# Macaron block: q and k projected transposed in two fp32r parts, head pairs on two 64-row halves, the causal mask added on VectorE, feed-forward loops unrolled

## The chip, the cores and the metric

One core of a Trainium2 chip (trn2) runs the whole program. The metric is device time in microseconds of that core. The kernel before took 1724.12 us, the median of 3 runs (1723.69 to 1725.47). Profiles are one further execution each.

## The reference

Three residual steps on x of 2 x 2048 tokens, 256 channels, all fp32:

```
x = x + 0.5 * ffn(layernorm(x))         # stage a
x = x + attention(layernorm(x))         # q, k, v projections are in stage a too
x = x + 0.5 * ffn(layernorm(x))         # stage c

ffn(x): h = relu(x @ W_fc.T)**2 (1024 wide); y = h @ W_proj.T
        mem = 0; five times: reset = mem > 1; mem = 0.9*mem + y - reset; spikes += mem > 1
        return spikes / 5
attention(x): 16 heads of 16; rope on q and k; scores = q k.T / 4, causal, softmax, @ v; then @ Wo.T + bo
```

The spikes are thresholds of y, so the products must be near fp32. The kernel therefore splits operands into a rounded high part and a rest and adds three products (high x high, high x low, low x high).

## The kernel before, in words

The program has three blocks, one after the other: `ffn_phase` with first=True (stage a), `attention_phase`, `ffn_phase` with first=False (stage c). DRAM tensors carry results between them.

**Feed-forward.** Tokens go in 8 chunks of 512 (4 tiles of 128, T). Each engine runs a software pipeline: `pipeline` calls body(n, has) for each chunk number, the middle of it as a hardware loop (Fori). A body has 8 turns f, one for each 128 of the 1024 hidden columns. On PE, turn f does `up` (6 matmuls of 512 columns, L569) and, three turns late (LAG), `down` (12 matmuls of 256 columns, L583). ScalarE takes relu and square (L313 to L322), VectorE subtracts the rounded part (h_lo, L450), counts spikes of the chunk before (L417) and does the layer norms (L376 to L399). Every engine executes in order; semaphores with the names in the wait calls tie them. In stage a the norm of the finished chunk ("mid"), its transposition (tps) and the projections stand in the same turns, placed by the table FROM: `qkv` projects one quarter (128 tokens) of q and k, 512 columns, then v, 256 columns, into one bank of gps; ScalarE copies it out; GpSimd rotates (rope, L520, L525) token-major; ScalarE and GpSimd and VectorE split it in three bf16 parts (L297, L546, L300, L474); PE transposes the parts in 48 matmuls of 128 columns a chunk (`fill`, L603), ScalarE copies these (L274) and issues their stores (L289). The pipeline is 5 turns of the outer loop deep, so it has 5 more bodies than chunks.

**Attention.** A group is four heads of one batch, 8 groups. Queries go in 4 steps j of 512, keys in blocks b of 128, so step j has 4j+4 blocks, 40 a group. On PE a block has: finds (L1066: q against up to 512 keys, into one of two buffers m_ps, read by VectorE's row maximum L983; 160 a group, and they run 20 blocks ahead of the scores), scores for head pairs (L1101, two matmuls of 512 columns into s_ps[hp], with the negated maximum as extra rows of q against rows of ones in k), and products with v (L1121, into o_ps; two block numbers behind; v_w is fp32 and the tile has 32 columns a head). Where the keys of a find end at the diagonal, an extra matmul (L1069) adds the mask. ScalarE does exp (L963), GpSimd zeroes above the diagonal (L936). Contraction rows: q and k have six part products of 16 rows, bf16, 96 rows (KR), and 3 rows of maxima parts. `place_units` distributes the 160 finds over block numbers -20 to 19 by cost. In a block, `some(quarter)` deals its finds in four portions; the order is some(0), scores 0, some(1), scores 1, some(2), products half 0, some(3), products half 1. A find waits until VectorE has read the buffer of the find two before.

The maxima of a step are negated and split (L992 to L1006), turned by PE (L1077), copied (L1014), and SP writes them to rows 96 to 98 of qT by three DMAs (`shift`, L873). SP also issues the loads of the next group's q and k (31 DMAs a group) and the stores.

Of the kernel before, what the change touches and what calls it, by code (L numbers as in the profile page):

```python
# [13 lines left out]
P = 128  # L14
# [20 lines left out]
QS, KS = (0, 0, 1, 1, 0, 2), (0, 1, 0, 1, 2, 0)  # L35
NT = len(QS)
KR = NT * D
KC = KR + 3
# [32 lines left out]
def ffn_phase(nc, first, src, dst, w, io, shared):  # L71
# [19 lines left out]
    with ExitStack() as ctx:  # L91
# [13 lines left out]
        ident, identb = sb("ident", [P, P]), sb("identb", [P, P], BF16)  # L105
# [13 lines left out]
        if first:  # L119
            xm = sb("xm", [P, T, E])  # L120
            mstats, mmv, mln = sb("mstats", [P, T, 6]), sb("mmv", [P, T, 2]), sb("mln", [P, 6, T])
            qk, rq, rest = (sb(n, [P, T, 2 * E]) for n in ("qk", "rq", "rest"))
            prod = sb("prod", [P, 4, E])
            parts = sb("parts", [P, T, 3, 2 * E], BF16)
            qkT = sb("qkT", [P, 12, CH], BF16)
            v = sb("v", [P, T, E])
            cosb, sinb = sb("cosb", [P, TOK // P, 2, D // 2]), sb("sinb", [P, TOK // P, 2, D // 2])

            staged = [rest[:, :, :].rearrange("p t n -> p (t n)"), qk[:, :, :].rearrange("p t n -> p (t n)"),
                      rq[:, 0:3, :].rearrange("p t n -> p (t n)")]  # L130
# [9 lines left out]
        gpsb = [gps[:, g, :].bitcast(BF16) for g in range(2)]  # L140
# [3 lines left out]
        names += ["const_in", "w_hi", "w_lo", "identb_ok", "x_in", "res_in", "up_done", "relu_done", "hi_done",  # L144
                  "sq_done", "lo_done", "down_done", "y_evac", "spike", "sum_done", "sum_out"]
        names += ["pre_" + n for n in norm_steps]
        if first:
            names += ["mid_" + n for n in norm_steps]
            names += ["qk_done", "qk_evac", "v_done", "v_evac", "v_out", "rope_mul", "rope_done",
                      "p0_done", "p1_done", "rest_done", "p2_done", "fill_done", "fill_evac", "qkT_out0", "qkT_out1"]  # L150
# [4 lines left out]
        passed, passed_dve, passed_sp, passed_act = (sem("passed" + x) for x in ("", "_dve", "_sp", "_act"))  # L155
        CONSTS = 16 * (3 if first else 2)

        FROM = {"qkv": 2, "rope": 3, "p0": 5, "rest": 6, "p1": 7, "fill": 8}
        FILLS = 2 * T
        FB = 12 // 2  # L160
# [9 lines left out]
        def turn_of(what, f):  # L170

            return (3 if f >= FROM[what] else 4), (f - FROM[what]) % FC

        def pipeline(eng, body):

            lo, hi, end = (5, NC - 1, NC + 5) if first else (3, NC - 2, NC + 3)
            for n in range(lo):
                body(n, lambda k: 0 <= n - k < NC)
            with eng.Fori(lo, hi) as it:
                body(it, lambda k: True)  # L180
            for n in range(hi, end):
                body(n, lambda k: 0 <= n - k < NC)
# [4 lines left out]
        def _(sp):  # L187
# [15 lines left out]
            if first:  # L203
                for tab, name in ((cosb, "cos"), (sinb, "sin")):
                    sp.dma_start(tab[:, :, :, :], w[name].rearrange("(t p) (k i) -> p t k i", p=P, k=2))\
                      .then_inc(s["const_in"], 16)
                load_weight(1)
                load_weight(2)

            def hold(name, value):  # L210

                if not isinstance(value, int) or value > 0:
                    sp.wait_ge(s[name], value)
                    if not isinstance(value, int):
                        sp.sem_inc(passed_sp, 1)

            def load_chunk(c):
                if first:
                    hold("pre_norm", c)
                else:  # L220
                    hold("a_T", c)
                    sp.dma_start(ain[:, :, :], rows(io["attn"], c)).then_inc(s["a_in"], 16)
                    hold("xb_done", c)
                sp.dma_start(xin[:, :, :], rows(src, c)).then_inc(s["x_in"], 16)

            def body(it, has):
                if has(-1 if first else -2):
                    load_chunk(it + (1 if first else 2))
                if has(2):
                    hold("sum_done", it - 2)  # L230
                    if not first:
                        hold("x2_out", 16 * (it - 1))
                    sp.dma_start(xres[:, :, :], rows(src if first else io["x2"], it - 2)).then_inc(s["res_in"], 16)
                if first and has(4):
                    hold("v_evac", T * (it - 3))
                    sp.dma_start(rows(io["v"], it - 4), v[:, :, :]).then_inc(s["v_out"], 16)
                if not first and has(-1):
                    hold("x2_done", it + 2)
                    sp.dma_start(rows(io["x2"], it + 1), x2[:, :, :]).then_inc(s["x2_out"], 16)
                if has(2):  # L240
                    hold("sum_done", it - 1)
                    sp.dma_start(rows(dst, it - 2), xsum[:, :, :]).then_inc(s["sum_out"], 16)

            if not first:
                load_chunk(1)
                wait(sp, "x2_done", 1)
                sp.dma_start(rows(io["x2"], 0), x2[:, :, :]).then_inc(s["x2_out"], 16)
            pipeline(sp, body)
            wait(sp, "sum_out", 16 * NC)
            if first:  # L250
                wait(sp, "v_out", 16 * NC)
                wait(sp, "qkT_out0", 48 * NC)
                wait(sp, "qkT_out1", 48 * NC)
# [4 lines left out]
        def _(act):  # L258
# [4 lines left out]
            def high(which, c, hi, bank=tps):  # L263

                wait(act, which + "_T", c + 1)
                act.activation(hi[:, :, :], bank[:, :, :], ACT.Copy).then_inc(s[which + "_hi"], 1)  # L266

            def fill_evac(c, i):

                t, half = divmod(i, 2)  # L270
                wait(act, "fill_done", FILLS * c + i + 1)
                if i in (0, T):
                    wait(act, f"qkT_out{i // T}", 48 * c)
                act.activation(qkT[:, FB * half:FB * (half + 1), t * P:(t + 1) * P],  # L274
                               gpsb[1][:, 0:FB * P].rearrange("p (k n) -> p k n", k=FB), ACT.Copy)\
                    .then_inc(s["fill_evac"], 1)

            def v_evac(c, t):
                wait(act, "v_done", T * c + t + 1)
                wait(act, "v_out", 16 * c)  # L280
                act.activation(v[:, t, :], gps[:, 0, 0:E], ACT.Copy).then_inc(s["v_evac"], 1)

            def store_parts(c, half):

                wait(act, "fill_evac", FILLS * c + T * (half + 1))
                act.sem_inc(passed_act, 1)
                n = CH // 2
                for a in range(3):
                    act.dma_start(io["qkT"][a].rearrange("(k p) n -> p k n", p=P)[:, :, bass.ds(c * CH + half * n, n)],  # L289
                                  qkT[:, 4 * a:4 * a + 4, half * n:(half + 1) * n]).then_inc(s[f"qkT_out{half}"], 16)  # L290

            def part(c, t, k):

                if k == 0:
                    wait(act, "rope_done", 2 * (T * c + t + 1))
                    wait(act, "fill_done", FILLS * (c - 1) + 2 * t + 2)
                    act.activation(parts[:, t, 0, :], rq[:, t, :], ACT.Copy).then_inc(s["p0_done"], 1)  # L297
                else:
                    wait(act, "rest_done", T * c + t + 1)
                    act.activation(parts[:, t, 1, :], rest[:, t, :], ACT.Copy).then_inc(s["p1_done"], 1)  # L300

            def body(it, has):
                for f in range(FC):
# [19 lines left out]
                    if first and has(2) and f == 5:  # L323
                        std("mid", it - 2, mln)
# [5 lines left out]
                    if first:  # L330
                        for which, what in enumerate(("p0", "p1")):
                            k, i = turn_of(what, f)
                            if f % 2 == 1 and has(k):
                                part(it - k, i // 2, which)
                        k, i = turn_of("qkv", f)
                        if f % 2 == 1 and has(k):
                            if i < FC - 1:
                                v_evac(it - k, i // 2)
                        elif has(k):
                            c, t = it - k, i // 2  # L340
                            wait(act, "qk_done", T * c + t + 1)
# [882 lines left out]
```

## Time and profile before

| what | value |
|---|---|
| runs | 1723.69, 1724.12, 1725.47 us |
| profiled execution | 1728.13 us, its span 1726.4 us |
| PE busy | 1505.3 us, 87% |
| PE weight loads busy | 828.1 us, 48% |
| VectorE (DVE) busy | 1200.0 us, 70% |
| ScalarE (ACT) busy | 947.9 us, 55% |
| GpSimd (POOL) busy | 353.9 us, 21% |
| mean granted TensorE clock | 0.933 of 2.4 GHz |

Busy shares are means over three stages. On the time line stage a ends near 411 us, attention proper begins at 504 us and ends near 1468 us, and stage c takes the rest. Idle of an engine that nobody waits for costs nothing; the prediction thus goes by stages and by who waits for whom.

### The profile page before, as it was taken

The page shows a single profiled execution, that of the slowest core. Times are in us where ns is not written, and L with a number is a line of the kernel's source. Part 1 is how long each engine was busy: PE and PEld are TensorE (multiplying, and loading weights), DVE is VectorE, ACT ScalarE, POOL GpSimd, SP SyncE. Part 2 cuts the span into 40 slices and gives each one's busy share as a digit, 9 for nine tenths or more (in the row PEclk, how much of TensorE's full clock was granted, in tenths as well). Part 3 has the DMA queues.
Part 4 walks back from the last instruction along what each step waited for, and adds up shares of the span by engine and source line. Part 5 has one row for each costly group of instructions (what it writes and reads, how often), then busy time and mean ns, then how long its engine had stood idle before and what let it go on. Part 6 is the DMA issues. An engine that isn't in the chain of part 4 may idle for free. (4 is left out here: it accounts for less than half of the span.)

```text
span 1726.4 us, 32516 instructions
## 1 busy us (share of the span) xinstructions
PE 1505.3 (87%) x11104; PEld 828.1 (48%) x11104; DVE 1200.0 (70%) x2269; ACT 947.9 (55%) x1332; POOL 353.9 (21%) x378
## 2 busy tenths in 40 slices
PE   5989888671489999998999989999999999599997
PEld 4877777551123333332333333333333333499996
DVE  4687766740478888886888877877887880366776
ACT  5656666562015555554555645555555568266654
POOL 0046656896001011011011020020010101101000
PEclk9999989885559999999999999999999999699999
DMA  4112222326352042052051070060150000322221
GB/s 117 60 39 71 83 73 74 105 79 122 37 62 32 5 62 36 5 73 26 5 79 19 5 94 5 5 93 5 19 81 6 4 8 5 111 74 86 97 73 62
DMA packets 130140, 90.54 MB, mean 52 GB/s; under 512 B 50625, under 2 KB 126401, under 8 KB 129985
## 3 DMA queue, kind: packets, MB, share of 16 engines
q1 hardware_dynamic: 104640, 75.92, 22.3%
q10 hardware_dynamic: 25344, 12.59, 2.4%
q8 instruction: 93, 1.52, 0.4%
q14 instruction: 63, 0.51, 0.1%
HBM read 54.53 MB, written 33.55 MB: 51 GB/s over the span
## 5 line engine op out<-in xcount | busy, mean ns | idle before, releaser
L983 DVE TENSOR_REDUCE maxes<-m_ps 128x1 f32<-128x512 f32 (+3 forms) x1280 | 743.6, 608 | 220.5 <-PE m_ps L1069 113.1
L963 ACT ACTIVATE probs<-s_ps 128x1024 f32<-128x1024 f32 (+3 forms) x640 | 540.8, 894 | 390.6 <-PE s_ps L1101 389.5
L1066 PE MATMUL m_ps<-kT,qT 96*128 96x512 bf16 (+3 forms) x1280 | 457.7, 369 | 102.3 <-DVE maxes L983 45.4
L1121 PE MATMUL o_ps<-probs,v_w 128*32 128x256 f32 (+2 forms) x4352 | 345.9, 393 | 0.3 <-POOL probs L936 0.3
L1101 PE MATMUL s_ps<-qT,kT 99*128 99x512 bf16 (+3 forms) x1280 | 341.1, 352 | 2.1 <-ACT probs L963 1.7
L1066 PEld LDWEIGHTS m_ps<-kT,qT 96*128 96x128 bf16 x1280 | 122.3, 97 | 443.4 <-DVE maxes L983 279.3
L936 POOL TENSOR_SCALAR_AFFINE_SELECT probs<-probs 128x512 f32<-128x512 f32 x128 | 81.3, 635 | 936.7 <-ACT probs L963 936.7
L1101 PEld LDWEIGHTS s_ps<-qT,kT 99*128 99x128 bf16 x1280 | 109.7, 99 | 107.1 <-issue 27.0
L1121 PEld LDWEIGHTS o_ps<-probs,v_w 128*32 128x32 f32 x4352 | 87.5, 108 | 132.5 <-issue 119.7
L1069 PE MATMUL m_ps<-maskb,identb_b 128*128 128x128 bf16 x512 | 116.6, 230 | 0.0
L520 POOL TENSOR_TENSOR prod_a<-qk_a,cosb_a 128x256 f32<-128x256 f32 x64 | 69.5, 1085 | 168.1 <-ACT qk_a L343 167.9
L450 DVE TENSOR_TENSOR h_lo_a<-hsq_a,h_hi_a 128x512 fp32r<-128x512 f32 x64 | 49.8, 780 | 68.7 <-ACT h_hi_a L322 68.7
L450 DVE TENSOR_TENSOR h_lo_c<-hsq_c,h_hi_c 128x512 fp32r<-128x512 f32 x64 | 51.4, 804 | 55.2 <-ACT h_hi_c L322 54.3
L313 ACT ACTIVATE relu_c<-ups_c 128x512 f32<-128x512 f32 x64 | 38.2, 596 | 76.5 <-PE ups_c L569 75.9
L611 PE MATMUL gps_a<-proj_hi_a,mT_hi_a 128*128 128x256 f32 (+1 forms) x128 | 51.2, 400 | 32.1 <-ACT qk_a L343 16.9
L313 ACT ACTIVATE relu_a<-ups_a 128x512 f32<-128x512 f32 x64 | 38.3, 598 | 69.3 <-PE ups_a L569 61.8
L583 PE MATMUL yps_a<-down_hi,h_hi_a 128*128 128x256 f32 x256 | 73.3, 286 | 2.6 <-ACT y_a L307 2.4
L583 PE MATMUL yps_c<-down_hi,h_hi_c 128*128 128x256 f32 x256 | 72.3, 282 | 0.0
L583 PE MATMUL yps_a<-down_lo,h_hi_a 128*128 128x256 f32 x256 | 71.9, 281 | 0.0
L583 PE MATMUL yps_c<-down_lo,h_hi_c 128*128 128x256 f32 x256 | 71.7, 280 | 0.0
L583 PE MATMUL yps_a<-down_hi,h_lo_a 128*128 128x256 f32 x256 | 71.6, 280 | 0.0
L583 PE MATMUL yps_c<-down_hi,h_lo_c 128*128 128x256 f32 x256 | 71.4, 279 | 0.0
(138 smaller groups left out, 2228.1 us busy)
## 6 DMA issues: line engine op xcount, KB each, us to landing
qkT_parts<-qkT_a ACTq DMA_DIRECT2D x48, 256.0 KB, 2.9
qT<-qkT_parts SPq DMA_DIRECT2D x192, 64.0 KB, 4.5
kT<-qkT_parts SPq DMA_DIRECT2D x48, 256.0 KB, 6.0
xin_a<-in_x SPq DMA_DIRECT2D x8, 512.0 KB, 4.2
xres_a<-in_x SPq DMA_DIRECT2D x8, 512.0 KB, 5.2
x<-xsum_a SPq DMA_DIRECT2D x8, 512.0 KB, 4.4
v_tok<-v_a SPq DMA_DIRECT2D x8, 512.0 KB, 3.0
v_in<-v_tok SPq DMA_DIRECT2D x8, 512.0 KB, 7.2
```

What stands on the lines that cost most here:

```text
L313: act.activation(relu[:, f % 2, :], ups[:, f % 2, :], ACT.Relu).then_inc(s["relu_done"], 1)
L450: dve.tensor_tensor(h_lo[:, f % HB, :], hsq[:, f % 2, :], h_hi[:, f % HB, :].bitcast(F32), ALU.subtract).then_inc(s["lo_done"], 1)
L520: pool.tensor_tensor(prod[:, 2 * half + m, :].rearrange("p (k h i) -> p k h i", k=2, h=H), x[:, :, :, :, m], table(tab), ALU.mult).then_in ...
L583: last = pe.matmul(yps[:, t, :], h[:, f % HB, t * P:(t + 1) * P], wt[:, f, :], start=(f == 0 and i == 0 and t % 2 == 0), stop=(f == FC - 1 ...
L611: last = pe.matmul(out, x[:, c, t * P:(t + 1) * P], wt[:, c, c0:c1], start=(i == 0), stop=(i == 3 * EC - 1))
L936: pool.affine_select(out=tile, in_=tile, compare_op=ALU.is_ge, fill=0.0, base=0, pattern=[[0, G], [1, P]], channel_multiplier=-1).then_inc ...
L963: act.activation(probs[:, b % PBUF, 2 * hp:2 * hp + 2, off:CH], s_ps[hp][:, :, off:CH], ACT.Exp)\
L983: dve.tensor_reduce(maxes[:, j % 2, h, t, k:k + 1], m_ps[:, u % 2, 0:width], AX.X, ALU.max)\
L1066: mm = pe.matmul(m_ps[:, u % 2, 0:width], q, kT[dn % 2][0:KR, h, k * CH:k * CH + width], start=True, stop=(k < j))
L1069: mm = pe.matmul(m_ps[:, u % 2, width - P:width], identb[:, :], maskb[:, :], start=False, stop=True)
L1101: mm = pe.matmul(s_ps[hp][:, h, off:CH], kT[dn % 2][0:KC, 2 * hp + h, b * P:(b + 1) * P], qT[dn % 2][0:KC, j, 2 * hp + h, off:CH], start=T ...
L1121: mm = pe.matmul(o_ps[VW * h:VW * (h + 1), start:end], v_w[dn % 2][:, b, h, :], probs[:, b % PBUF, h, start:end], start=(b == 0), stop=(b ...
```

## The change

- Stage a: q and k are projected transposed (weights stationary, tokens moving, 512 columns): first q's two halves of head dimensions, then k's, then v as before. VectorE multiplies by cos and sin from a table (`rot`, 128 x 3 x 2048), GpSimd adds and subtracts, ScalarE rounds to fp32r, GpSimd subtracts the rest. No PE transposition of q and k remains. SP stores all parts, as fp32.
- Attention: q and k have two parts, three products of 16 rows, 48 rows, in fp32r, and 2 rows of maxima parts. Heads of a pair lie at partitions 0 and 64 (HR = 64). The mask is a [128, 512] tile; a diagonal find's maximum is one VectorE operation that adds it and takes the maximum. The scale of 1/4 is in the exp. VectorE transposes the maxima in 32 x 32 blocks; 16 DMAs put them in place.
- The products of a block are one piece of up to 512 columns instead of two halves with a find between.
- Both feed-forward loops are unrolled; SP's loads and stores are in another order. Stage a's pipeline has 3 more bodies than chunks.

```
-QS, KS = (0, 0, 1, 1, 0, 2), (0, 1, 0, 1, 2, 0)
+QS, KS = (0, 0, 1), (0, 1, 0)
 KR = NT * D
-KC = KR + 3
+KC = KR + 2
...
         def pipeline(body):
+            for n in range(NC + (3 if first else 2)):
                 body(n, lambda k: 0 <= n - k < NC)
...
     SP, start of stage a: cos and sin loads leave; after the weights:
+                sp.dma_start(table[:, :, :], w["rot"]).then_inc(s["table_in"], 16)
...
     PE, stage a:
+            def project_pair(c, x):
+                if x == 0:
+                    wait(pe, "mid_evac", c + 1)
+                    wait(pe, "v_evac", c)
                 else:
+                    wait(pe, "turn_done", 4 * c + 2)
+                for ab in range(2):
+                    n0 = (2 * x + ab) * P
+                    (six matmuls: gps[:, ab, :] <- wt[:, k, n0:n0 + P], x_[:, k, :])
+            def project_v(c):
+                wait(pe, "turn_done", 4 * c + 4)
+                for t in range(T):
+                    last = project(gps[:, t // 2, (t % 2) * E:(t % 2 + 1) * E], t, 2 * E, 3 * E)
...
+                    f == 0: project_pair(it - 3, 1)    (behind down, ahead of up(it, 0))
+                    f == 3: project_v(it - 3)
+                    f == 4: wait mid_norm; turn(xm, "mid_T")
+                    f == 6: project_pair(it - 2, 0); then turn(xn)
...
     VectorE, stage a:
+            def turn_pair(c, x):
+                wait(dve, "proj_done", 3 * c + x + 1)
+                wait(dve, "rot_done", 4 * c + 2 * x)
+                for m in range(2):
+                    dve.tensor_tensor(turned[:, m], gps[:, :, :], table[:, m:m + 2, t0:t0 + CH], ALU.mult)
+                    f == 1: mid statistics;  f == 2: turn_pair(it - 3, 1), last in its turn
+                    f == 3: mid norm;  f == 5: low mid;  f == 7: turn_pair(it - 2, 0), last in its turn
...
     GpSimd, stage a:
+            def rotate(c, x):   two subtract/add of 128x512, then qk_lo (128x1024)
...
     attention, VectorE:
+                if k < j:
+                    dve.tensor_reduce(out, m_ps[:, u % 2, 0:width], AX.X, ALU.max).then_inc(max_read, 1)
+                else:
+                    dve.wait_ge(max_read, FREE_M + len(UNITS) * n + u - 1)
+                    dve.sem_inc(passed_max, 1)
+                    dve.tensor_tensor_reduce(masked[:, u % 2, 0:width], m_ps[:, u % 2, 0:width], mask[:, CH - width:CH], 1.0, NEG,
+                                             ALU.add, ALU.max, out).then_inc(max_read, 1)
...
     attention, PE:
-                if k == j:
-                    mm = pe.matmul(m_ps[:, u % 2, width - P:width], identb[:, :], maskb[:, :], start=False, stop=True)
+                pe.matmul(m_ps[:, u % 2, 0:width], qT[dn % 2][r0:r0 + KR, j, h // 2, t * P:(t + 1) * P],
+                          kT[dn % 2][r0:r0 + KR, h // 2, k * CH:k * CH + width], start=True, stop=True)
...
-                    for half in range(2):
-                        if b >= 2:
-                            products(i, dn, j, b - 2, half)
-                        if half == 0:
-                            some(3)
+                    if b >= 2:
+                        products(i, dn, j, b - 2)
+                    some(3)
...
     attention, SP:
+                for a in range(2):
+                    for par in range(2):
+                        for r in range(P // VW):
+                            sp.dma_start(out[:, :, r, :].bitcast(F32), shiftT[c0:c0 + G * T // 2, :]).then_inc(shift_in, 16)
-                    load(i, dn + 1, (2 * j, 2 * j + 1))
+                    load(i, dn + 1, (j,))
...
     attention, start: VectorE sets rows of kT[0] to 1 and the mask to 0; SP waits for both
+            sp.wait_ge(ones_ok[0], 2)
             load(0, 0, range(NT))
```

## Rows read from the trace of the kernel before

**Rows 1.** Windows, attention: us, PE, PEld, DVE, ACT, POOL busy, PEclk, DMA

```profile
604.00:690.00 86.00, 82.63 (x674) 30.43 (x673) 70.03 (x134) 50.54 (x62) 9.95 (x13) 1.00 0.35 49
```

**Rows 2.** Order of time, ScalarE, stage a: start us, us, engine, line, operation

```profile
237.44 1.03 ACT L307 ACTIVATE y_a<-yps_a 128x1024 f32<-128x1024 f32 x1
...
282.50 1.03 ACT L307 ACTIVATE y_a<-yps_a 128x1024 f32<-128x1024 f32 x1
...
320.91 1.03 ACT L307 ACTIVATE y_a<-yps_a 128x1024 f32<-128x1024 f32 x1
```

**Rows 3.** Order of time, SP and PE, from stage a to the first score

```profile
411.65 0.35 SPq L848 DMA_DIRECT2D ident_b<-in_ident  x1
...
447.50 0.26 PE L1066 MATMUL m_ps<-kT,qT 96*128 96x128 bf16 x1 [41.45 <-DMA kT<-qkT_parts]
...
504.63 0.63 PE L1101 MATMUL s_ps<-qT,kT 99*128 99x512 bf16 x1
```

**Rows 4.** Chain that ended last, stage c: start us, us, what

```profile
1506.54 2.75 PE ups_c L569 x12
...
1522.19 2.83 PE yps_c L583 x24
```

**Rows 5.** Order of time, PE, one full key block

```profile
809.14 0.39 PE L1066 MATMUL m_ps<-kT,qT 96*128 96x512 bf16 x1
...
810.45 0.38 PE L1066 MATMUL m_ps<-kT,qT 96*128 96x512 bf16 x1
...
810.76 0.64 PE L1121 MATMUL o_ps<-probs,v_w 128*32 128x256 f32 x8
...
811.33 0.39 PE L1066 MATMUL m_ps<-kT,qT 96*128 96x512 bf16 x1
...
812.28 0.39 PE L1066 MATMUL m_ps<-kT,qT 96*128 96x512 bf16 x1
```

**Rows 6.** Order of time, PE and DVE, a block with a whole product

```profile
586.02 1.06 PE L1121 MATMUL o_ps<-probs,v_w 128*32 128x512 f32 x8
587.02 0.50 PE L1066 MATMUL m_ps<-kT,qT 96*128 96x512 bf16 x2
...
587.45 1.02 DVE L983 TENSOR_REDUCE maxes<-m_ps 128x1 f32<-128x512 f32 x2 [0.89 <-PE m_ps L1066]
588.19 0.39 PE L1066 MATMUL m_ps<-kT,qT 96*128 96x512 bf16 x1 [0.62 <-DVE maxes L983]
...
588.62 2.00 DVE L983 TENSOR_REDUCE maxes<-m_ps 128x1 f32<-128x512 f32 x3
```

**Rows 7.** DMA issues (KB each, us to landing); order of time, DVE, start

```profile
rest_a<-in_up SPq DMA_DIRECT2D x1, 1024.0 KB, 6.6
...
26.63 1.40 DVE L376 BATCH_NORM_STATS2 stats_a<-xin_a 128x6 f32<-128x256 f32 x4
```

**Rows 8.** Order of time, ScalarE and DVE, stage c, turn f = 7

```profile
1577.21 0.60 ACT L313 ACTIVATE relu_c<-ups_c 128x512 f32<-128x512 f32 x1 [1.88 <-PE ups_c L569]
...
1580.50 1.22 DVE L417 SCALAR_TENSOR_TENSOR count_c<-y_c,count_c 128x1024 bf16<-128x1024 f32 x1
```

**Rows 9.** Forms of instructions: out<-in xcount | busy us, mean ns | idle before

```profile
L983 DVE TENSOR_REDUCE maxes<-m_ps 128x1 f32<-128x512 f32 x896 | 600.7, 689 | 138.4 <-PE m_ps L1066 92.7 <-PE m_ps L1069 34.3
...
L546 POOL TENSOR_TENSOR rest_a<-rq_a,parts_a 128x512 f32<-128x512 f32 x32 | 41.3, 1293 | 9.1 <-ACT parts_a L297 9.1
...
L434 DVE TENSOR_TENSOR x_c<-gps_c,xb_c 128x1024 f32<-128x1024 f32 x8 | 9.8, 1225 | 11.9 <-PE gps_c L611 11.9
```

**Rows 10.** Line L873 (min/median/max ns); order of time around a shift

```profile
L873 SPq DMA_DIRECT2D qT<-shiftT x96: 502/582/1659, 468.3 to 1428.8; - x96
DMA to landing us min/median/max: 1.6/1.7/3.2
...
687.95 0.17 DVE L1006 TENSOR_TENSOR negparts<-negrest,negparts 128x16 bf16<-128x16 f32 x1
...
698.62 0.60 PE L1101 MATMUL s_ps<-qT,kT 99*128 99x512 bf16 x2
```

More of the change, by code:

```diff
@@ L153, in ffn_phase @@
         s = {n: sem(n) for n in names}
[L155 to L160, printed above, removed]
+        passed_dve = sem("passed_dve")
+        CONSTS = 16 * (1 if first else 2)
         def rows(ap, c):
@@ L168, in wait, with pipeline @@
                 eng.wait_ge(s[name], value)
[L170 to L181, printed above, removed]
+        def pipeline(body):
+            for n in range(NC + (3 if first else 2)):
                 body(n, lambda k: 0 <= n - k < NC)
@@ L244, in _, with load_x, load_attn @@
[L244 to L248, printed above, removed]
+                sp.dma_start(table[:, :, :], w["rot"]).then_inc(s["table_in"], 16)
+            def load_x(c):
+                wait(sp, "pre_norm" if first else "xb_done", c)
+                sp.dma_start(xin[:, :, :], rows(src, c)).then_inc(s["x_in"], 16)
+            def load_attn(c):
+                wait(sp, "a_T", c)
+                sp.dma_start(ain[:, :, :], rows(io["attn"], c)).then_inc(s["a_in"], 16)
@@ new lines, in load_rest, with store_sum, store_x2 @@
+            def load_rest(c):
+                wait(sp, "sum_done", c)
+                if not first:
+                    wait(sp, "x2_out", 16 * (c + 1))
+                sp.dma_start(xres[:, :, :], rows(src if first else io["x2"], c)).then_inc(s["res_in"], 16)
+            def store_sum(c):
+                wait(sp, "sum_done", c + 1)
+                sp.dma_start(rows(dst, c), xsum[:, :, :]).then_inc(s["sum_out"], 16)
+            def store_x2(c):
+                wait(sp, "x2_done", c + 1)
+                sp.dma_start(rows(io["x2"], c), x2[:, :, :]).then_inc(s["x2_out"], 16)
@@ L265, in high @@
                 wait(act, which + "_T", c + 1)
+                if which == "mid":
+                    wait(act, "proj_done", 3 * c)
                 act.activation(hi[:, :, :], bank[:, :, :], ACT.Copy).then_inc(s[which + "_hi"], 1)
[L268 to L276, printed above, removed]
@@ L292, in part, with v_evac @@
[L292 to L300, printed above, removed]
+            def v_evac(c):
+                wait(act, "proj_done", 3 * c + 3)
+                wait(act, "v_out", 16 * c)
+                act.activation(v[:, :, :], gps[:, :, :].rearrange("p g (t e) -> p (g t) e", e=E), ACT.Copy)\
+                    .then_inc(s["v_evac"], 1)
@@ L659, in body @@
                         up(it, 0)
-                    if first and f == 0 and has(4):
-                        qkv(it - 4, FC - 1)
-                    if first and f == 0 and has(3):
-                        wait(pe, "mid_norm", it - 2)
-                        turn(xm, "mid_T")
                     if not first and f == 5 and has(-2):
@@ L1157, in body @@
                     for b in (last - 2, last - 1):
-                        for half in range(2):
-                            products(i, dn, j, b, half)
+                        products(i, dn, j, b)
                     turn_sum(i, dn, j, True)
-            pe.wait_ge(const_ok, 2)
-            pe.wait_ge(ones_ok, 6)
+            pe.wait_ge(const_in, 32)
             for x in range(MAX_FROM, 0):
```

488 lines of the change are left out of this document (208 added, 280 removed).

## The prediction

> **What bounds the kernel now.** I read the page first, then windows, chain, forms and time-ordered instructions. TensorE is the page's busiest engine, but its reasons differ by stage. In 86 us of the attention VectorE (DVE in the rows) is busy 70 and PE nearly all of the time [rows 1]. A full key block shows a closed cycle on PE: find at 809.14, find at 810.45, half products, find with mask, half products, next block's find at 812.28, thus 3.14 us [rows 5]. (A find is the 512-column score matmul whose row maximum VectorE takes.) A find stands between the two half products, and VectorE has only two m_ps buffers to read from. Where a product is already whole (the first key block of a query step), the reader sees another order: the product holds PE 1.00 us, VectorE stands 0.89 us, and PE's following find then waits 0.62 us for VectorE [rows 6].
>
> The first stage runs until 411.65, although its last feed-forward result is read at 320.91: a tail of 90.7 us. Its chunks take 45.1 us apiece late in the loop [rows 2, 3], while feed-forward matmuls alone would need 8 x (1.38 + 1.41) = 22.3 us per chunk [rows 4]. Then 35.9 us pass until attention's first find, and 57.1 us more until its first score [rows 3]. The last feed-forward stage follows PE's chain and keeps its arithmetic.
>
> The profiled execution took 1728.1 us for a span of 1726.4; the median of the runs is 1724.1, thus 4 us less. Differences worked out in the span are applied to the median.
>
> **Start, +6.** Cosine and sine loads of 0.25 MB each, and the wait of PE and ScalarE for them, leave; that is worth about 2 us. A 3.1 MB table is put on SP's queue before chunk 1's x. A 1 MB weight load took 6.6 us with 0.5 MB ahead of it [rows 7], thus about 230 GB/s at best: 3.1 MB is 14 us. VectorE takes the chunk's statistics at 26.6 us [rows 7], and what is queued up to it totals 7 MB, 31 us or more. Behind this wait stand the remaining h_lo subtractions of VectorE, and behind those PE. Net +6, bounds 0 and +14.
>
> **First stage, loop, -16.** PE per chunk afterwards: feed-forward 22.3, the q and k pairs 24 matmuls of 512 columns at 0.23 = 5.5, v 24 of 256 at 0.118 = 2.8, sixteen transposes about 2.0: 32.7 us. The 48 small transposes and their ScalarE copies leave. But only one PSUM pair serves all three projections. The second pair waits for VectorE's rotation products of the first, queued at f = 7 behind low, h_lo and a spike count. In the last stage the same queue can be read: the relu after up(7) starts at 1577.21, the spike count at 1580.50 [rows 8]. The count costs 1.14 and two 1024-element products (1.225 each [rows 9], a little overlapped) 2.4: done, with 0.2 from matmul to relu, 7.1 us after up(7). PE has two down groups, 2.8 us, in the meantime and stands 4.3. The v projection waits for the second pair's rotation, queued behind sum and both norms' statistics: about 2.5. The y copy adds 0.8. Period 32.7 + 7.6 = 40.3 against 45.1. Five chunks have this form, of which the last is cheaper before as well (38.4), and the first of them is slightly dearer: I take 16 us, bounds 0 and 30. Unrolling removes only loop branches, less than 2 us per turn, and is inside this.
>
> **First stage, tail, -37.** After the last y: count and norm of chunk 6 and 7, two transposes, two pairs and two rotations for each. Walked by order: y to chunk 6's second rotation 22 us, norm of 7 and transposes and splits 8, first pair 5 (at 1.2 GHz), rotation 2.4, second pair 5, rotation 2.4, GpSimd's two 512-column steps 2.4 (1.29 each at most [rows 9]), high part 1.0, low part 2.4, four DMA issues and landing 4. About 53 to 54 us against 90.7, since the token-major rope (six GpSimd operations per quarter chunk) is gone. Bounds -20 and -50. GpSimd is not busy enough in the loop to matter.
>
> **Boundary, -1.** 31 loads become 19 with rows of 2 and 8 KB in place of 1 and 4; bytes stay 3.6 MB. They filled most of 35.9 us before. Now VectorE must first set 2 x 4096 elements of kT (at the element rate of the adds in rows 9 4.3 us each, 9.2 with the mask) and SP stands behind it. With 25 us for the loads the sum is 35, bounds -9 and +9.
>
> **Finds ahead of the first score, -3.** Of the 57.1 us [rows 3]: no mask matmuls, ScalarE copies or PE turn of the shift; bounds -8 and +5.
>
> **Attention proper, +30.** This is the largest term. The numbers follow find d, the one after the product: VectorE starts 0.43 later (587.02 to 587.45). Its reductions follow each other every 0.655 (three in 2.00, one being 0.69) and each holds its buffer 0.69. Find c of the next block starts 0.05 after find a's reduction ends (588.14 to 588.19) [rows 6, 9]. From find to product 0.31, product to find 1.00 [rows 5, 6]. With four finds per block: 0.43 + 0.655 + 0.69 + 0.05 + 0.31 + 1.00 = 3.14 us. So the merged product gives back everything that PE saves, whatever the score pairs cost. With five finds there are two behind the product: 3.79, against 3.14 + 0.23 = 3.37 before. Per head group: four such blocks, +1.7. Fp32r finds at 0.23 instead of 0.215 lie beside. Some ten blocks with few finds stay bound by PE and gain one switch, the mask and perhaps parallel scores, about 0.25 each: -2.5. Masked maxima: 64 per group, half on the cycle, each with a further semaphore instruction and an accumulator. No row shows this custom operation. A PSUM plus SBUF add of 1024 elements takes 1.225 us, so 512 take 0.69, as the reduction does [rows 9]: lower bound 0 extra (less is excluded, it reads the same columns). Upper bound is a second small VectorE operation and its spacing, 0.35 (the subtraction of 0.17 and its spacing of 0.2 [rows 10]). I take 0.15, near to the small operation's duration: 64 x 0.5 x 0.15 = +4.8. Sum +4.0 per group, and 7.5 groups run with finds: +30. Bounds: 105 less (rival A) and 90 more (rival B).
>
> A rule speaks against the masked maxima. The Trainium skill, VectorE: DVE Perf Modes, section Two Vector instructions with no wait between them, says that an operation that also writes its accumulator is two instructions. No run here shows it. It is what the slower rival would be.
>
> **Shifts, +4.** Three DMAs become sixteen, at 0.50 to 0.58 us an issue [rows 10]. For the last query step the parts are ready at 688.1 and the first score starts at 698.6 [rows 10]. Sixteen issues and 1.7 landing are 9.7 to 11.0 us, in a window of 10.5, perhaps a little shorter now. PE's whole queue stands behind it. 0 to 1.5 us, eight times: +4, bounds 0 and +12. The two loads and one store that share SP's queue have gone out before.
>
> **Rest, -2.** In the last 20 blocks without finds ScalarE's two exponentials set the pace, -1. Final stage: the same PE order, -1; if its hidden loads come late, +5.
>
> **Sum.** 6 - 16 - 37 - 1 - 3 + 30 + 4 - 2 = -19; 1724 - 19 = **1705 us**.
>
> **Rival A, packing pays.** Two 64-row score matmuls run at once, and the finds too; then PE would need 4 x 0.23 + 2 x 0.23 + 1.0 + 0.2 = 2.6 us per block. For it: the eight product instructions of four 32-column tiles end in 0.57 us, so tiles do overlap here [rows 5]. Against it: the cycle above holds no score, and the already whole products stand with VectorE idle. If find latency proves less than 0.43 or finds slip beside products, 0.5 us x 7.5 x 28 blocks = 105 less: 1705 - 105 = 1600. Chance 0.12. The Trainium skill, TensorEngine Tiling (Array Packing), section Theoretical Speedup, allows up to 2x for at most 64 rows; the 0.57 us agree that packing occurs.
>
> **Rival B, slower.** VectorE's masked maximum is dear. Place: L983's 512 diagonal units. Break-even: 19 us over 7.5 x 32 = 240 on the cycle, 0.08 beyond my 0.15, so from 0.23 each. At 0.35: 240 x 0.20 = +48, 1753 us. For it: an added instruction, an added wait and a second output. Against: VectorE idles 16 of 86 us [rows 1], which hides extras off the cycle. If three quarters of the 480 lie on it at 0.35, 126 us in place of 36: +90, 1795. Chance 0.27.
>
> **Rival C, the first stage gives nothing.** Its new waits (4.3 and 2.5) grow by a missed turn of the in-order queues, and the table delays more. Loop and start then cost instead of give: 20 us back, 1725. Chance 0.13. The forecast has 0.48.
>
> **Range and chances.** A measurement cannot tell changes under 0.2%, 3.4 us. Forecast alone: 1685 to 1722. The range, 1640 to 1775, takes in most of B and the near side of A. Faster: A 0.12, forecast 0.44, C 0.03, thus 0.59. Same: C 0.06, forecast 0.02. Slower: B 0.27, C 0.04, forecast 0.02, thus 0.33.
>
> **What would show it.** Phase 1 ends near 365, chunks of 40 us, PE waiting at the second pair and the v projection. First find near 400. In full blocks VectorE idle about 0.8 us behind each whole product, though PE waits for maxes. Masked maximum of 512 columns at about 0.7 to 0.85. Wrong if blocks fall under 2.9 us, if masked maxima exceed 0.95, or if the tail keeps more than 70 us.

## The result and the profile after

The kernel after takes 2059.2 us (2050.6 to 2065.1, 4 runs) where the one before took 1724.4: a ratio of 1.194, 95% interval 1.189 to 1.198. The forecast was 1705, the range ended at 1775: wrong in sign and far outside. The profiled run took 2065.1 us for a span of 2063.3.

The page of the profile after, part 1, two rows of part 2 (tenths of busy time and of the granted TensorE clock in 40 slices):

```profile
PE 1750.3 (85%) x8384; PEld 941.1 (46%) x8384; DVE 1196.7 (58%) x2719; ACT 869.6 (42%) x1160; POOL 220.9 (11%) x202
...
PE   6888787249989998988989888998899999869997
...
PEclk9999898655555756665665655577575565879999
```

The clock row of before, from its page:

```profile
PEclk9999989885559999999999999999999999699999
```

PE is as busy as before by its share, but the clock row stands at 5 to 7 from the eighth slice to the 34th. Before, only the three slices ahead of the first scores had a 5, and those from the 13th to the 34th a 9. PE's busy time in the span grew from 1505 to 1750 us, although 2,720 of its instructions are gone. So PE works at 1.2 GHz, the lower of the two levels, for most of the attention. Windows by stage (us, busy time of PE, PEld, DVE, ACT, POOL, PEclk, DMA share, GB/s):

```profile
0.00:382.00 382.00, 297.94 (x1664) 259.61 (x1664) 249.82 (x451) 164.48 (x261) 85.49 (x51) 0.92 0.31 100
382.00:450.00 68.00, 10.53 (x21) 5.72 (x21) 16.99 (x44) 0.44 (x1) 15.72 (x8) 0.50 0.58 81
450.00:1790.00 1340.00, 1202.56 (x5132) 467.39 (x5135) 772.77 (x1942) 557.45 (x659) 95.39 (x131) 0.60 0.18 24
```

The attention has 0.60 in place of the 1.00 of [rows 1] (0.99 from 600 to 1400 us of before). Instructions in order of time, after: the bounds of the stages on SP and PE, a full key block at 1.2 GHz, and the wait for the last shift.

```profile
390.63 0.36 SPq L796 DMA_DIRECT2D ident_b<-in_ident  x1
400.17 0.36 SPq L798 DMA_DIRECT2D mask_b<-in_mask  x1
...
435.83 0.48 PE L1021 MATMUL m_ps<-kT,qT 48*128 48x128 f32 x2 [55.39 <-DMA qT<-qkT_parts]
...
498.23 1.12 PE L1041 MATMUL s_ps<-qT,kT 50*128 50x512 f32 x2
...
732.39 1.93 PE L1058 MATMUL o_ps<-probs,v_w 128*32 128x512 f32 x8
734.26 0.79 PE L1021 MATMUL m_ps<-kT,qT 48*128 48x512 f32 x2
734.85 0.63 PE L1041 MATMUL s_ps<-qT,kT 50*128 50x512 f32 x2
735.84 0.79 PE L1021 MATMUL m_ps<-kT,qT 48*128 48x512 f32 x1 [0.36 <-DVE maxes L943]
735.92 1.14 PE L1041 MATMUL s_ps<-qT,kT 50*128 50x512 f32 x2
736.51 0.72 PE L1021 MATMUL m_ps<-kT,qT 48*128 48x512 f32 x1
737.15 1.93 PE L1058 MATMUL o_ps<-probs,v_w 128*32 128x512 f32 x8
...
1767.03 1.22 PE L1041 MATMUL s_ps<-qT,kT 50*128 50x512 f32 x4 [5.88 <-DMA qT<-shiftT]
```

The whole product holds PE 1.87 us instead of 1.00, and the block takes 4.76 us (732.39 to 737.15) in place of 3.14 [rows 5]. The score pair starts 0.08 us behind a find (735.84, 735.92): matmuls in different 64-row halves do overlap. VectorE's part, by forms (count, busy us, mean ns, idle before):

```profile
L943 DVE TENSOR_REDUCE maxes<-m_ps 128x1 f32<-128x512 f32 x768 | 510.0, 688 | 250.6 <-PE m_ps L1021 246.2
...
L948 DVE CUSTOM_DVE_ANT_0 masked<-m_ps,mask_b 128x512 f32<-128x512 f32 x128 | 86.9, 690 | 83.7 <-PE m_ps L1021 82.0 <-DVE maxes L943 0.3
...
L948 DVE DVE_READ_ACCUMULATOR2_ANT maxes<- 128x1 f32 x512 | 42.5, 83 | 0.0
```

Reductions cost what they did [rows 9]; most of VectorE's idle time before them now ends with PE (246.2 of 250.6 us). Cut at PE's first score and at PE's first transposition of the last stage, the two profiled spans compare as follows (us):

| | before | after | difference |
|---|---|---|---|
| start to last y | 320.9 | 332.1 | +11.2 |
| last y to end of the first stage | 90.7 | 58.6 | -32.1 |
| to the first find | 35.9 | 45.2 | +9.3 |
| to the first score | 57.1 | 62.4 | +5.3 |
| attention, first score to last stage | 974.0 | 1315.4 | +341.4 |
| last stage | 247.8 | 249.7 | +1.9 |

Everything ahead of the attention nets -6. The question is the 341.

### The profile page after: what moved, and what is told of

It is laid out like the page before. It is cut to its first block and busy times, and to the rows that moved or that the text cites. A ratio compares the mean times of both kernels' runs of the same rounds, so it can differ in the third digit from the quotient of the medians.

```text
span 2063.3 us, 27094 instructions
## 1 busy us (share of the span) xinstructions
PE 1750.3 (85%) x8384; PEld 941.1 (46%) x8384; DVE 1196.7 (58%) x2719; ACT 869.6 (42%) x1160; POOL 220.9 (11%) x202
## 5 line engine op out<-in xcount | busy, mean ns | idle before, releaser
L1021 PE MATMUL m_ps<-kT,qT 48*128 48x512 f32 (+3 forms) x1280 | 662.2, 643 | 189.2 <-DVE maxes L943 61.8
L943 DVE TENSOR_REDUCE maxes<-m_ps 128x1 f32<-128x512 f32 x768 | 510.0, 688 | 250.6 <-PE m_ps L1021 246.2
L1021 PEld LDWEIGHTS m_ps<-kT,qT 48*128 48x128 f32 x1280 | 284.3, 262 | 796.7 <-DVE maxes L943 282.8
L1058 PE MATMUL o_ps<-probs,v_w 128*32 128x512 f32 (+3 forms) x2560 | 467.4, 818 | 0.2 <-POOL probs L895 0.2
L1041 PE MATMUL s_ps<-qT,kT 50*128 50x512 f32 (+3 forms) x1280 | 452.1, 552 | 7.9 <-DMA qT<-shiftT 5.9
L948 DVE CUSTOM_DVE_ANT_0 masked<-m_ps,mask_b 128x384 f32<-128x384 f32 (+3 forms) x512 | 244.9, 490 | 315.0 <-PE m_ps L1021 305.0
L1041 PEld LDWEIGHTS s_ps<-qT,kT 50*128 50x128 f32 x1280 | 223.2, 273 | 31.1 <-ACT probs L918 22.2
L1058 PEld LDWEIGHTS o_ps<-probs,v_w 128*32 128x32 f32 x2560 | 59.8, 129 | 105.3 <-issue 78.8
L436 DVE TENSOR_TENSOR h_lo_c<-hsq_c,h_hi_c 128x512 fp32r<-128x512 f32 x64 | 45.0, 703 | 62.2 <-ACT hsq_c L310 35.7
L494 POOL TENSOR_TENSOR rot_a<-turned_a 128x512 f32<-128x512 f32 x32 | 46.9, 1484 | 176.8 <-DVE turned_a L420 176.8
L574 PE MATMUL gps_a<-mT_hi_a,proj_hi_a 128*128 128x512 f32 x64 | 33.3, 520 | 33.8 <-DVE turned_a L420 29.0
```

The source lines that it names most:

```text
L436: dve.tensor_tensor(h_lo[:, f % HB, :], hsq[:, f % 2, :], h_hi[:, f % HB, :].bitcast(F32), ALU.subtract).then_inc(s["lo_done"], 1)
L494: pool.tensor_tensor(rot[:, x, m, :], turned[:, m, 0, :], turned[:, m, 1, :], op)\
L943: dve.tensor_reduce(out, m_ps[:, u % 2, 0:width], AX.X, ALU.max).then_inc(max_read, 1)
L948: dve.tensor_tensor_reduce(masked[:, u % 2, 0:width], m_ps[:, u % 2, 0:width], mask[:, CH - width:CH], 1.0, NEG, ALU.add, ALU.max, out).th ...
L1021: pe.matmul(m_ps[:, u % 2, 0:width], qT[dn % 2][r0:r0 + KR, j, h // 2, t * P:(t + 1) * P], kT[dn % 2][r0:r0 + KR, h // 2, k * CH:k * CH + ...
L1041: mm = pe.matmul(s_ps[hp][:, h, off:CH], kT[dn % 2][HR * h:HR * h + KC, hp, b * P:(b + 1) * P], qT[dn % 2][HR * h:HR * h + KC, j, hp, off: ...
```

## Experiments

Theory R: a matmul over 48 to 50 rows of the array leaves the granted clock low, where 96 to 99 rows raise it. Rivals: theory T (fp32r operands in place of bf16) and theory G (PE's gaps, made by whole products and VectorE). "Low" below is the time at 1.2 GHz in the attention, summed over windows of 10 us from their PEclk; "attention" is cut as in the table above. Before has 31 us low and 974.0; after 1015 low and 1315.4. Another start of the windows moves "low" by some 10 us. Where a pair of numbers is in brackets behind a ratio, it is the 95% interval.

**Run 1, 96 rows in one tile.** The row group of each pair's second head moves from row 64 to row 48, the shifts to rows 96 and up. What comes out is the attention of the sum of two heads' scores, and two matmuls no longer lie in different halves of the array.

```
-  r0 = HR * (h % 2);  q, k rows r0:r0 + KR              # finds, 48 rows
+  q, k rows 0:96
-  rows HR * h:HR * h + KC                               # scores, 50 rows
+  rows 0:98
```

> The kernel after, with both heads of a pair in one full-height tile: finds contract 96 rows (48 of each head) and scores 98, where after they contract 48 and 50 in a 64-row half. Number type (fp32r), instruction counts, waits and loads stay; what is computed is the attention of the sum of the two heads' scores, so the output is another one. Theory R (the granted TensorE clock falls because finds and scores fill few rows of the array): the clock of the attention rises from about 0.60 to 0.95 or more, and the time falls from 2059 to 1735 to 1790 us. Theory T (it falls because the operands are fp32r in place of bf16) and theory G (it falls because PE has gaps around the whole product and the masked maxima): clock stays near 0.6, time 2040 to 2080 us.

Measured: 1835.7 us (1828.7 to 1844.1); attention 1102.5, low 123. Its window:

```profile
600.00:1400.00 800.00, 726.83 (x3783) 364.67 (x3781) 567.42 (x1409) 412.69 (x485) 72.45 (x98) 0.95 0.26 33
```

With 96 and 98 rows the clock is back and 224 us of the loss are gone. T falls as the main cause, since this is fp32r. So does G, since the products are whole and the maxima masked. The rows and the packing changed together here; run 2 changes the rows in unpacked tiles. The expected time was missed by 46 us; run 12 takes that up.

**Run 2, before with 48 rows.**

```
-QS, KS = (0, 0, 1, 1, 0, 2), (0, 1, 0, 1, 2, 0)
+QS, KS = (0, 0, 1), (0, 1, 0)
```

> The kernel before, with three of its six terms of q and k left out: finds contract 48 rows and scores 51 in place of 96 and 99, in bf16, full-height tiles, half the loads; the scores are less exact. Theory R (few rows): the granted clock of the attention falls from 0.99 to about 0.6 and the time rises to 1950 to 2060 us. Theories T (fp32r) and G (gaps): clock stays at 0.95 or more, time 1705 to 1730 us.

Measured: 2433.2 us (2430.3 to 2445.7), attention 1678.5, low 1613. Its windows, and PE in order of time:

```profile
600.00:1400.00 800.00, 793.11 (x3484) 212.12 (x3481) 372.68 (x711) 268.33 (x307) 44.98 (x63) 0.50 0.08 13
```

```profile
803.65 1.08 PE L1123 MATMUL o_ps<-probs,v_w 128*32 128x256 f32 x8
804.67 0.60 PE L1068 MATMUL m_ps<-kT,qT 48*128 48x512 bf16 x1
...
806.44 0.60 PE L1068 MATMUL m_ps<-kT,qT 48*128 48x512 bf16 x1
806.84 1.06 PE L1103 MATMUL s_ps<-qT,kT 51*128 51x512 bf16 x2
...
809.53 1.08 PE L1123 MATMUL o_ps<-probs,v_w 128*32 128x256 f32 x8
```

R holds, and neither rival: bf16, half products, the mask matmuls, PE busy 793 of 800 us, and a clock of 0.50. The time lies far above the expected 1950 to 2060, for which I had only scaled after. A block takes 5.88 us (803.65 to 809.53), since here the score pair starts 0.40 behind the find and not 0.08. Run 2 also differs from after by its mask matmul (about 0.2) and its half products; run 3 takes the products out of the comparison.

**Run 3, after with half products.** The halves and the finds between them as before.

> The kernel after, with each product again in two halves and the last quarter of the finds between them. Theory G (gaps of PE around whole products): the clock of the attention goes back to 0.95 or more, time 1700 to 1760 us. Theories R (rows) and T (type): clock stays near 0.6; the halves add eight short instructions where PE is the bound, time 2050 to 2120 us.

Measured: 2140.4 us (2104.5 to 2154.5; the runs spread too far for an interval), attention 1408.4, low 1314. Attention and low are those of the slowest run, whose clock over the whole span is 0.64; the fastest run has 0.67. PE in order of time:

```profile
804.99 1.08 PE L1061 MATMUL o_ps<-probs,v_w 128*32 128x256 f32 x8
806.00 0.79 PE L1021 MATMUL m_ps<-kT,qT 48*128 48x512 f32 x1
...
810.03 1.08 PE L1061 MATMUL o_ps<-probs,v_w 128*32 128x256 f32 x8
```

G falls here too: half products leave the clock low in every run. A block takes 5.04 us (804.99 to 810.03), 0.28 more than with a whole product, and 0.84 less than in run 2. Less the mask matmul, overlap of the halves of the array is worth some 0.6 us a block at 1.2 GHz, an estimate, since the two runs also differ in number type.

**Run 4, before with whole products.**

> The kernel before, with whole products and the last finds behind them. The prediction's closed cycle (0.43 from a find's start to VectorE, 0.655 a reduction, product 1.00) gives 3.14 us for blocks with four finds, as before, and 3.79 for those with five in place of 3.37, and 0.2 less in blocks bound by PE: together 1720 to 1750 us, clock 0.95 or more. Theory G (gaps drop the clock): clock near 0.6, time over 1950 us. If packing or slack hides the cycle (rival A's ground): 1700 to 1718 us.

Measured: 1735.7 us, ratio 1.007 (1.005 to 1.009), attention 981.0, low 34. PE, then DVE, in order of time:

```profile
807.24 1.07 PE L1118 MATMUL o_ps<-probs,v_w 128*32 128x512 f32 x8
...
810.44 1.07 PE L1118 MATMUL o_ps<-probs,v_w 128*32 128x512 f32 x8
```

```profile
805.52 2.52 DVE L983 TENSOR_REDUCE maxes<-m_ps 128x1 f32<-128x512 f32 x4 [0.67 <-PE m_ps L1069]
```

Blocks of 3.20 us with VectorE idle 0.67 to 0.69 in each: the closed cycle of the prediction (3.14, 0.8). It costs 7 us in the attention. G falls once more: whole products, and 34 us low.

**Run 5, hybrid.** First stage of after, attention of before; each rotated pair is split in three bf16 parts (ScalarE, GpSimd, ScalarE, GpSimd) in place of two fp32r parts.

> The first stage of the kernel after with the attention of the kernel before: q and k projected transposed, but split in three bf16 parts for 96-row finds and 99-row scores. The first stage of after ends 21 us earlier than before's (390.6 against 411.65); the third part adds one ScalarE copy and one GpSimd subtraction per pair, some 5 to 8 us in the tail and little in the loop. If the clock theory of rows holds, the attention is that of before: clock 0.98, time 1705 to 1720 us. If the loss of after came from its first stage or its loads: over 1724 us.

Measured: 1745.6 us, ratio 1.011 (1.009 to 1.013). The attention is before's again (973.0 us), but the time was missed by 26 us: chunks of the first stage took 49 to 51 us apiece against 45.

**Run 6, before with zero rows.** The terms of run 2, the tiles of before.

```
+  memset qT, kT rows 0:96 to 0 once;  LOADS of three terms (rows 0:48)
   finds contract 96 rows, scores 99
```

> The kernel before with three of its six terms, the other 48 rows filled with zeros in q and k: finds contract 96 rows and scores 99, half of them zero. The same numbers are computed as in the run with 48 rows, and the scores are less exact than before's. If rows count whatever they hold (theory R as stated): clock near 0.98 in the attention, 1725 to 1765 us, part of it for the filling ahead of the attention. If only rows with data count: clock 0.5 to 0.6, 2350 to 2450 us, as with 48 rows.

Measured: 1735.3 us, ratio 1.004 (1.002 to 1.006), attention 974.7, low 43. Its windows beside run 2's:

```profile
600.00:1400.00 800.00, 762.58 (x6162) 283.53 (x6162) 636.37 (x1249) 454.15 (x546) 79.96 (x110) 0.98 0.12 22
```

The cleanest pair of the study: the same loads and the same sums, 48 rows against 96 of which 48 are zero; clock 0.50 against 0.98, 2433 against 1735 us. In this pair it is the number of rows that the instruction spans that counts, and not what they hold. Rows alone are not enough, though: before's finds ahead of its first score contract 96 rows and stay at 0.50.

**Run 7, hybrid with y ahead of the root.**

> The same with ScalarE's square root of the second norm queued behind the copy of y instead of ahead of it. In after the copy stands behind that root, which waits for VectorE's statistics; PE waits 3.9 us for the copy in each chunk and then starts at 1.2 GHz. If this order is what costs, five chunks give back 3 to 5 us each: 12 to 20 us less than the run above, 1690 to 1705 us. If VectorE is late anyway: the same time within 3 us.

Measured: 1745.8 us, no change where 12 to 20 us less were expected. In the hybrid ScalarE's copy was late for another reason. In order of time, run 7, ScalarE and GpSimd:

```profile
269.67 1.06 ACT L290 ACTIVATE qkp_a<-rot_a 128x1024 bf16<-128x1024 f32 x1 [4.27 <-POOL rot_a L502]
```

```profile
263.87 2.85 POOL L510 TENSOR_TENSOR qkp_a<-rot_a,qkp_a 128x1024 bf16<-128x1024 f32 x1 [17.67 <-ACT qkp_a L294]
266.67 2.97 POOL L502 TENSOR_TENSOR rot_a<-turned_a 128x512 f32<-128x512 f32 x2
```

GpSimd waits 17.7 us for a middle part that ScalarE takes only in the next turn, then rotates late; ScalarE, in order, stands 4.3 us ahead of y.

**Run 8, after with 62 and 64 rows.** 14 zero rows fill each half.

> The kernel after, each 64-row half filled up: 14 rows of zeros in q (ones in k) between the three terms and the shift, so that finds contract 62 rows and scores 64, in the same two halves that PE overlaps. The same numbers are computed. If the rows that a matmul spans keep the clock up, and two overlapped halves count together: clock 0.9 or more in the attention and 1740 to 1850 us, which would be the packed kernel at 2.4 GHz. If 62 rows are still too few: clock 0.6 to 0.75, 1950 to 2070 us.

Measured: 1880.1 us, ratio 1.090 (1.087 to 1.094), attention 1127.3, low 382. Its window:

```profile
600.00:1400.00 800.00, 682.60 (x3643) 270.93 (x3640) 539.41 (x1373) 394.37 (x468) 67.75 (x93) 0.82 0.25 32
```

It lies between the two answers: 14 zero rows give back 179 us and 62% of the low time. A line through after and this run (188 us of attention for 633 us low) put on before's 31 us low gives some 1023 us, an estimate: with the clock held, the packed attention would still be about 50 us behind before's, and some 290 of after's 341 us would be the clock's.

**Run 9, before with masked maxima.** VectorE adds the mask as it takes the maximum; the mask matmul is gone.

> The kernel before with the mask added by VectorE as it takes the maximum of a diagonal unit, in place of the mask matmul: this edit alone, at 2.4 GHz. The prediction took 0.15 us for each of 64 per head group, half on the cycle, against 0.05 us of PE each for the mask matmul: -2 to +3 us per group, together 1715 to 1745 us. Rival B (dear masked maxima, 0.35 us each): 1745 to 1800 us. If the clock hangs on the mask matmuls: clock near 0.6, over 1950 us.

Measured: 1727.9 us, ratio 1.002 (1.001 to 1.003), attention 974.1. With half products, and with the mask matmuls gone in exchange, masked maxima cost nothing in the attention.

**Run 10, the middle part in its own turn.**

```
-  if f == 0 and has(4): part_mid(it - 4, 1)
+  if f == 7 and has(3): part_mid(it - 3, 1)
```

> The hybrid with y ahead of the root, with ScalarE's middle part of k moved from the start of the next turn to f=7 of its own, so that GpSimd's last subtraction of a chunk no longer holds up the next rotation. In the hybrid ScalarE stood 4.2 us for that rotation in every chunk and its chunks took 51 us against 45 in after. If this queue is the cause: chunks of 44 to 47 us, 1705 to 1722 us. If it is something else: 1740 us or more.

Measured: 1731.1 us, ratio 1.003 (1.002 to 1.004). Chunks fall from 51.1 to 47.4 us, a little short of the 44 to 47 expected, and the time misses the expected 1722 by 9 us.

**Run 11, the second pair behind up and down.**

```
-  if first and f == 0 and has(3): project_pair(it - 3, 1)    # ahead of up(it, 0)
+  if first and f == 1 and has(3): project_pair(it - 3, 1)
```

> The same, with the second projected pair (k) at f=1 behind up and down in place of f=0 ahead of up: 4 us of other matmuls lie between the first pair and the second, where PE waited 4.1 us for VectorE's rotation products. If that wait and the clock of 1.2 GHz behind it go, five chunks give 4 to 6 us each: 1680 to 1705 us. If the wait only moves to the v projection or to y: within 5 us of the run above.

Measured: **1693.1 us** (1690.3 to 1695.5), ratio **0.981** (0.979 to 0.983). It is faster than both kernels, than before by 1.9%. Two copies of y, then SP at the end of the first stage:

```profile
232.93 1.00 ACT L301 ACTIVATE y_a<-yps_a 128x1024 f32<-128x1024 f32 x1
273.27 1.01 ACT L301 ACTIVATE y_a<-yps_a 128x1024 f32<-128x1024 f32 x1
```

```profile
377.56 0.36 SPq L813 DMA_DIRECT2D ident_b<-in_ident  x1
```

This chunk takes 40.3 us (those beside it 38.8 and 41.1), the first stage ends 34 us ahead of before's, and the attention is before's (972.4, low 35).

**Run 12, run 1 with half products.**

> The run with 96 and 98 rows in one tile (attention of the sum of two heads' scores, 1835.7 us) with each product in two halves again and the last quarter of the finds between them. It stands 111 us above before, though the granted clock is back: 123 us of its attention are at 1.2 GHz against 31, and a full block takes 3.4 us where before's takes 3.14. If whole products are what leaves gaps and low clock: 1735 to 1780 us and under 60 us at 1.2 GHz. If it is the dearer fp32r weight loads (200 ns against 97): 1815 to 1860 us, since the halves add four of the products' own loads.

Measured: 1858.5 us, ratio 1.079 (1.074 to 1.083), attention 1116.5, low 187. Halves are not what run 1 lacked. Run 1, forms of the weight loads, and a full block in order of time:

```profile
L1019 PEld LDWEIGHTS m_ps<-kT,qT 96*128 96x128 f32 x1280 | 245.7, 203 | 535.5 <-DVE maxes L941 244.3 <-DVE maxes L946 190.5 <-issue 80.7
```

```profile
836.42 1.06 PE L1056 MATMUL o_ps<-probs,v_w 128*32 128x512 f32 x8
...
838.69 0.50 PE L1019 MATMUL m_ps<-kT,qT 96*128 96x512 f32 x1
839.03 0.64 PE L1039 MATMUL s_ps<-qT,kT 98*128 98x512 f32 x2
...
839.82 0.64 PE L1056 MATMUL o_ps<-probs,v_w 128*32 128x512 f32 x4
```

A find and its score lie 0.34 us apart, not the 0.22 to 0.23 of run 4, and the block takes 3.40 in place of 3.14 or 3.20: an fp32r weight load takes 203 ns where before's bf16 loads took 97 (means over all finds), and part of it is not hidden. If 0.2 us is lost in some 150 of the 320 blocks, a number that was not counted, that is about 30 us; of the 89 us more at low clock than in run 4 half is lost, 45. Together, as an estimate, 75 of run 1's 121 us over run 4. The rest, and why the clock falls more often here than in before, I have not split.

## Why the prediction was wrong, point by point

**The step that failed is "Attention proper, +30".** It says "from find to product 0.31, product to find 1.00" and adds up a cycle from durations of [rows 5, 6], all of them rows at PEclk 1.00, and sets that "fp32r finds at 0.23 instead of 0.215 lie beside". No term, bound or rival of this step allowed the clock itself to change. The matmuls of finds and scores got half as many rows; runs 2 and 6 show that this takes the clock from 0.98 to 0.50 in before's tiles, and in after's halves it is 0.60. The attention cost +341, of which some 290 are the clock's by the line of run 8, an estimate; the 50 that it leaves are near the +34 forecast for the attention and its shifts. The page could have raised the question: its clock row has a 5 where finds of 96 rows run alone ahead of the first score, busy as PE is there (43.6 of 57 us), and I did not ask what would keep the clock up after the change.

The Trainium skill, TensorE: Matmul & The Clock Gate, section Part 1: The HAM clock gate, says that activity releases the throttle and speaks of how busy the PE has been. Run 2 was busy 793 of 800 us at 0.50, so busy time as the profile counts it does not decide here. Between runs 2 and 6, the rows spanned do.

**The cycle itself was right.** Run 4 gives 3.20 us against 3.14 and VectorE idle 0.69 against 0.8; the edit costs 7 us in the attention. **Masked maxima** take 0.69 plus 0.083 us each, within the bounds. In run 9 they cost 0 us in the attention instead of 36 (240 on the cycle at 0.15), but run 9 keeps before's half products. In after's own order, at 2.4 GHz, the block at 1409.28 holds two of them and takes 3.49 us, the one before it holds none and takes 3.30; those at 790.60 and 793.89 hold two and take 3.29 and 3.30. So they are hidden in some blocks and cost about 0.1 us each in others; the sum over the attention was not measured. The Trainium skill, VectorE: DVE Perf Modes, section Two Vector instructions with no wait between them, is confirmed by the 512 accumulator reads. **fp32r** was mis-sized too: a find and its score lie 0.34 us apart in run 1 in place of 0.23, which I put down to the dearer weight load; no run has that alone.

**Start, +6:** -2 by the first y. The first y comes at 49.5 against 51.5, VectorE's statistics of chunk 1 at 24.0 against 26.6. I took 230 GB/s as the best rate from one load's landing; the windows of the first 20 us show 349.

**Loop, -16:** +13. The wait at the second pair was right (4.07 against 4.3). The v projection waits for nothing. The copy of y costs 3.9, not 0.8. In the trace of after the root of the second norm stands right ahead of it, at 256.75 against 256.87; run 7 could not test this order alone, since another wait covered it in the hybrid. And behind each such wait the clock is at 1.2 GHz: the twelve matmuls behind the first start 0.43 us apart in place of 0.23, until about 246. After, PE, in order of time:

```profile
239.98 0.79 PE L574 MATMUL gps_a<-mT_hi_a,proj_hi_a 128*128 128x512 f32 x1 [4.07 <-DVE turned_a L420]
240.57 0.63 PE L574 MATMUL gps_a<-mT_lo_a,proj_hi_a 128*128 128x512 f32 x1
240.99 0.63 PE L574 MATMUL gps_a<-mT_hi_a,proj_lo_a 128*128 128x512 f32 x1
...
257.92 0.58 PE L543 MATMUL yps_a<-down_hi,h_hi_a 128*128 128x256 f32 x1 [3.85 <-ACT y_a L297]
```

Chunks thus take 45 us, not 40.3, and they are heavy one chunk earlier than before's. Rival C (the first stage gives nothing) came true for the loop. Run 11, which puts 4 us of matmuls into the first wait, has 40.3 us in one chunk, but this is no proof of the sum: it has three bf16 parts, y ahead of the root, and a wait of up to 3.8 us for the norm ahead of its transposition that the sum did not have.

**Tail, -37:** -32 (58.6 us against 53 to 54; the parts listed there add up to 54.6): the mechanism was right. **Boundary, -1:** +9.3, just past its bound of +9. SP stands 9.2 us for VectorE's fills (390.63 to 400.17), as forecast; the loads were mis-sized, at 35.7 us (400.17 to 435.83) in place of 25. **Finds ahead, -3:** +5.3, just past its bound of +5. **Shifts, +4:** 5.9, but in a single wait, at the last query step of the last group (1767.03), and not 0 to 1.5 us eight times; that the sum is near is luck. **Rest, -2:** +1.9.

**Rival A** (packing pays) has its mechanism and not its price: overlap saves some 0.6 us a block at 1.2 GHz, where PE is the bound. At 2.4 GHz VectorE's cycle stands over it, as a stretch of after shows in which the clock is 1.00. PE, then DVE, in order of time:

```profile
1405.98 1.06 PE L1058 MATMUL o_ps<-probs,v_w 128*32 128x512 f32 x8
...
1408.26 0.50 PE L1021 MATMUL m_ps<-kT,qT 48*128 48x512 f32 x1 [0.55 <-DVE maxes L943]
...
1409.28 1.06 PE L1058 MATMUL o_ps<-probs,v_w 128*32 128x512 f32 x8
```

```profile
1407.51 1.98 DVE L943 TENSOR_REDUCE maxes<-m_ps 128x1 f32<-128x512 f32 x3 [0.73 <-PE m_ps L1021]
```

The packed block takes 3.30 us with VectorE idle 0.73 and PE waiting for it: the cycle of the forecast, and not the 2.6 of the rival. Of after's blocks at 2.4 GHz with four finds of 512 columns, the shortest takes 2.87. **Rival B**'s price of 0.35 us each, on three quarters of the masked maxima or on half, is borne out by no run: the dearest of the blocks read above show about 0.1. **Still open:** what fp32r does to the clock at equal rows beyond run 1 against run 4 (123 against 34 us low), why the clock comes back in parts of after, and what besides the rows keeps it at 0.50 ahead of the first score.

## What to carry to other kernels

A duration read in a trace holds only for its granted clock: where an edit shrinks the rows that matmuls contract, price the stage at both levels, or keep the rows up with zeros. In run 6 these cost 0.7 us of attention against before, and filling them 8 us ahead of it. Packing two heads into halves of the array saves PE time that a VectorE-bound cycle doesn't need, and can lose the clock for it. A wait of PE of some 4 us costs twice in this kernel, its length and the slow matmuls behind it: fill it with work that is ready (38 us for one moved line, run 11 against run 10).

## What the runs showed of the hardware that was not expected

- 48 of 96 contracted rows set to zero: clock 0.98; the same 48 rows alone: 0.50. In 64-row halves, 48 and 50 rows gave 0.60, 62 and 64 rows 0.82, between 600 and 1400 us of each span.
- Before's finds ahead of the first score contract 96 rows, PE is busy 43.6 of 57 us, and the clock is 0.50.
- fp32r weight loads of 128 columns take 203 ns (run 1) against 97 for bf16 (before), means over all finds.
- One VectorE operation seems to wait for GpSimd: a 1.22 us count takes 3.41 beside a GpSimd subtraction, and ends 1.1 us behind its end, in five chunks alike. A shorter subtraction of VectorE (0.68 us) in the same stretch is not longer than elsewhere, so it isn't every operation (after, VectorE and GpSimd in order of time).

```profile
274.53 1.22 DVE L390 SCALAR_TENSOR_TENSOR count_a<-y_a,count_a 128x1024 bf16<-128x1024 f32 x1
...
276.27 3.41 DVE L390 SCALAR_TENSOR_TENSOR count_a<-y_a,count_a 128x1024 bf16<-128x1024 f32 x1
```

```profile
275.66 2.93 POOL L499 TENSOR_TENSOR qk_lo_a<-rot_a,qk_hi_a 128x1024 fp32r<-128x1024 f32 x1 [12.52 <-ACT qk_hi_a L290]
```
